# 16-head attention of the last layer: the maximum and its subtraction taken straight from PSUM by VectorE, without a copy of the scores and without GpSimd

## The chip, the cores and the metric

The kernel runs on one core of a Trainium2 chip. The metric is the device time of one execution in microseconds (us), the median of several runs. Five engines of the core work side by side, each through a queue of its own in program order, and they wait for one another through semaphores: PE (TensorE, the matrix engine), DVE (VectorE), ACT (ScalarE), POOL (GpSimd) and SP (SyncE, which issues transfers). SBUF is the on-chip memory, PSUM the memory into which PE writes its results, in 8 banks. POOL works on tiles in SBUF here and never on PSUM.

## The reference

The model has four layers, each a cross attention and a feed-forward part, over x of 2 x 512 x 128. The context has 2 x 77 x 128. Layer L2 (with a mask) and layer L3 (without one) use the same 16-head attention. L3, cut to what matters:

```python
def _L3_xattn_ref(query, key, value, Wq, bq, Wk, bk, Wv, bv, Wo, bo):
    H, D_K = 16, 8
    def proj(x, W, b):
        y = jnp.einsum('bsd,df->bsf', x, W) + b
        return y.reshape(B, -1, H, D_K).transpose(0, 2, 1, 3)
    q, k, v = proj(query, Wq, bq), proj(key, Wk, bk), proj(value, Wv, bv)
    scores = jnp.einsum('bhqd,bhkd->bhqk', q, k) / jnp.sqrt(jnp.float32(D_K))
    p = jax.nn.softmax(scores, axis=-1)
    x = jnp.einsum('bhqk,bhkd->bhqd', p, v)
    x = x.transpose(0, 2, 1, 3).reshape(B, -1, H * D_K)
    return jnp.einsum('bsd,df->bsf', x, Wo) + bo
...
x = x + _L3_xattn_ref(_layernorm(x, axis=-1), ctx_1024, ctx_1024, ...)
```

## The kernel before

Each engine has one function that writes out its whole program; nothing is scheduled by a planner, so the order on each queue is the order in which the code is written. `attention16(n, k)` stands once on each engine's side and is called twice: with n = 0 for L2 (mask) and n = 1 for L3 (no mask). It treats the 1024 queries in NT = 8 tiles of 128 rows. Batch b is t // 4. The scores of one tile are 16 heads x 77 keys = 1232 numbers in each of the 128 rows. They are computed as float32 split into high and low halves, three groups of four matmuls (L1091), and they fill banks 0 to 3 with 308 columns each.

What one tile goes through with n = 1:

- PE `scores(t)` writes banks 0 to 3. There is one such set of banks, so `scores(t + 1)` may begin only when `s16_taken` says that tile t has been copied away.
- DVE copies the 1232 columns to an SBUF tile `s16[z]` (L1944; three of them by turns; the profile calls them `shared` or `scratch`), counts `s16_taken`, and takes the negated maximum of each head from that SBUF copy into `neg_max16` (L1946), counting `max16_ok`.
- POOL `less_maximum` adds the negated maximum to `s16[z]` (L696) and counts `s16_ok`. With n = 0 a small operation on the maxima comes before (L694).
- ACT takes the exponential in two pieces (L1489, L1491; the profile calls the output `hT`).
- PE turns it in ten transposes (L1106, L1111), ACT copies these out (L1502, L1506; `w` in the profile), PE makes the weighted averages (L1122, L1126), ACT copies (L1479), PE turns back (L1134), DVE divides by the sum of the exponentials (L1956, L1959).

PE's queue works ahead of this by three tiles. First `scores(0)`, `scores(1)`, `scores(2)`, each of the last two behind a wait for the previous tile; then a loop over t, whose iteration is: wait for `s16_taken` of tile t + 2, `keep_warm(0, 1)` (one matmul of ones of 512 columns, two rows of 128x512 in the profile under L461, written to bank 0 and never used; its only purpose is to keep PE busy), `scores(t + 3)`, `averages(t - 1)`, `transposes(t)`, `turn_back(t - 1)`. In iteration 5 there are no scores left, but the wait for the last tile stays. Below, tile numbers are counted from 0, and "the filler" is the matmul of `keep_warm`.

Of the kernel before, what the change touches and what calls it, by code (L numbers as in the profile page):

```python
# [5 lines left out]
ALU = mybir.AluOpType  # L6
ACT = mybir.ActivationFunctionType
AX = mybir.AxisListType
# [5 lines left out]
P = 128  # L14
B = 2
NT = 8
# [20 lines left out]
def build(nc, a, out):  # L37
    S = a["x"].shape[1]
    D = a["x"].shape[2]
    NC = a["ctx_1024"].shape[1]  # L40
# [16 lines left out]
    BK = HM // 4  # L57
# [7 lines left out]
    with ExitStack() as ctx:  # L65
# [43 lines left out]
        for n in VROWS:  # L109
            k = vsrc[n].shape[0] // D  # L110
# [100 lines left out]
        s16 = [v.rearrange("p (h k) -> p h k", h=HM) for v in  # L211
               (scratch[:, 0:HM * NC], scratch[:, HM * NC:2 * HM * NC], shared[:, mask_at:mask_at + HM * NC])]
# [312 lines left out]
        def _(pool):  # L525
# [159 lines left out]
                            .then_inc(kv16_spread, 1)  # L685
                        nc.gpsimd.tensor_copy(to_left[:, :, :, DH], row_of).then_inc(kv16_spread, 1)

            def less_maximum(t, n):

                z = (NT * n + t) % 3  # L690
                pool.wait_ge(max16_ok, NT * n + t + 1)
                if n == 0:

                    own.add(nc.gpsimd.tensor_scalar(neg_max16[:, z, :], neg_max16[:, z, :], 1e37, None, ALU.min))  # L694
                    own.settle()
                nc.gpsimd.tensor_tensor(s16[z], s16[z], neg_max16[:, z, :].unsqueeze(2).to_broadcast([P, HM, NC]), ALU.add)\  # L696
                    .then_inc(s16_ok, 1)

# [30 lines left out]
            add_bias(4, bo16[:, 0, :])  # L729

            for t in range(NT):
                less_maximum(t, 0)
            spread_kv(1)
            inverse_root(5)

# [5 lines left out]
                    .then_inc(gu_product_ok, 1)  # L741
            inverse_root(6)
            add_bias(6, bo16[:, 1, :])
            for t in range(NT):
                less_maximum(t, 1)
            inverse_root(7)

        @block.tensor
        def _(pe):
# [322 lines left out]
            def attention16(n, k):  # L1072


                norm_transposes(k)

                def queries_of(b):
                    pe.wait_ge(xnT_b_ok[b], k)
                    nc.tensor.matmul(bank[:, 6 + b, :], w16[:, n, WQ, :], xnT[:, b, :], start=True, stop=True)\
                        .then_inc(q16_in_psum, 1)  # L1080

                def scores(t):
                    b, m = t // TPB, NT * n + t
                    pe.wait_ge(q16_ok, B * n + b + 1)
                    if t:
                        pe.wait_ge(s16_taken, m)
                    for stationary, moving in ((HI, HI), (HI, LO), (LO, HI)):
                        begin, end = stationary == moving, stationary == LO
                        for g in range(4):
                            rows = slice(32 * g, 32 * (g + 1))  # L1090
                            last = nc.tensor.matmul(bank[:, g, 0:BK * NC],  # L1091
                                                    qT[stationary][rows, b, (t % TPB) * P:(t % TPB + 1) * P],
                                                    k_blocks[moving][rows, b].rearrange("p h k -> p (h k)"),
                                                    start=begin, stop=end)
                    last.then_inc(s16_in_psum, 1)

                def transposes(t):

                    m, z = NT * n + t, t % 2
                    pe.wait_ge(p16_ok, 2 * (m + 1))  # L1100
                    if t:
                        pe.wait_ge(p16T_ok, 2 * m)
                    else:
                        pe.wait_ge(q16_ok, B * (n + 1))
                    for c in range(NPAIR):
                        last = nc.tensor.transpose(bank[:, 4 + c // 4, (c % 4) * P:(c % 4 + 1) * P],  # L1106
                                                   p16[:, z, 2 * PK * c:2 * PK * (c + 1)], ident[:])
                    last.then_inc(p16T_in_psum, 1)
                    for g in range(2):
                        first = HM * PK + LP * g  # L1110
                        last = nc.tensor.transpose(bank[0:LP, 6, g * P:(g + 1) * P], p16[:, z, first:first + LP],  # L1111
                                                   ident[:])
                    last.then_inc(p16T_in_psum, 1)

                def averages(t):

                    b, m = t // TPB, NT * n + t
                    pe.wait_ge(p16T_ok, 2 * m + 2)
                    if m >= 1:
                        pe.wait_ge(o16_ok, m)  # L1120
                    for g in range(2):
                        nc.tensor.matmul(bank[:, 7, g * P:(g + 1) * P], va_left[:, n, b, g, :], p16T[0:LP, NPAIR + g, :],  # L1122
                                         start=(g == 0), stop=False, skip_group_check=True)
                    for c in range(NPAIR):
                        g, rows = c // 4, slice(VW * (c % 4), VW * (c % 4 + 1))
                        last = nc.tensor.matmul(bank[rows, 7, g * P:(g + 1) * P], va_pair[:, n, b, c, :], p16T[:, c, :],  # L1126
                                                start=False, stop=(g == 1), skip_group_check=True)
                    last.then_inc(oT16_in_psum, 1)

                def turn_back(t):  # L1130

                    pe.wait_ge(oT16_ok, NT * n + t + 1)
                    for g in range(2):
                        last = nc.tensor.transpose(bank[:, 7, (2 + g) * P:(3 + g) * P], oT16[:, g, :], ident[:])  # L1134
                    last.then_inc(o16_in_psum, 1)

                def output_transposes(b):
                    for t in range(TPB * b, TPB * (b + 1)):
                        pe.wait_ge(o16_ok, NT * n + t + 1)
                        last = nc.tensor.transpose(bank[:, b, (t % TPB) * P:(t % TPB + 1) * P], o16[:, t, :], ident[:])  # L1140
                    last.then_inc(o16T_in_psum, 1)

                def output(b):
                    pe.wait_ge(o16T_ok, B * n + b + 1)
                    result_part(b, (3, 7)[b], lambda t: q16T[:, t // TPB, (t % TPB) * P:(t % TPB + 1) * P],
                                w16[:, n, WO, :])

                queries_of(0)
                keep_warm(4, 1)
                queries_of(1)  # L1150
                pe.wait_ge(kv16_spread, 7 * B * (n + 1))
                for t in range(3):
                    scores(t)
                for t in range(NT + 1):
                    if t + 3 < NT:
                        pe.wait_ge(s16_taken, NT * n + t + 3)
                        keep_warm(0, 1)
                        scores(t + 3)
                    elif t == NT - 3:
                        pe.wait_ge(s16_taken, NT * (n + 1))  # L1160
                        keep_warm(2, 1)
                    elif t == NT - 2:
                        output_transposes(0)
                        keep_warm(2, 1)
                    elif t == NT - 1:
                        output(0)
                        keep_warm(2, 1)
                    else:
                        keep_warm(2, 2)
                    if t:  # L1170
                        averages(t - 1)
                    if t < NT:
                        transposes(t)
                    if t:
                        turn_back(t - 1)
                keep_warm(2, 1)
                output_transposes(1)
                output(1)
# [416 lines left out]
        def _(dve):  # L1595
# [323 lines left out]
            def attention16(n, k, result):  # L1919
# [12 lines left out]
                for t in range(NT + LAG):  # L1932
                    m, z = NT * n + t, (NT * n + t) % 3
                    if t < NT:
                        scores, to = bank[:, 0:4, 0:BK * NC], s16[z].rearrange("p (g h) k -> p g (h k)", g=4)
                        dve.wait_ge(s16_in_psum, m + 1)
                        if m >= 3:
                            dve.wait_ge(p16_ok, 2 * (m - 2))
                        if n == 0:
                            nc.vector.scalar_tensor_tensor(out=to, in0=maskb[:, t, :].rearrange("p (g n) -> p g n", g=4),  # L1940
                                                           scalar=MASKED, in1=scores, op0=ALU.mult, op1=ALU.add)\
                                .then_inc(s16_taken, 1)
                        else:
                            nc.vector.tensor_copy(to, scores).then_inc(s16_taken, 1)  # L1944
                        dve.wait_ge(s16_taken, m + 1)
                        nc.vector.tensor_reduce(neg_max16[:, z, :], s16[z], AX.X, ALU.max, negate=True)\  # L1946
                            .then_inc(max16_ok, 1)
                    if t >= LAG:

                        d, y = NT * n + t - LAG, (t - LAG) % 2  # L1950
# [199 lines left out]
```

## Time and profile before

| | us |
|---|---|
| median of 3 runs | 504.54 |
| lowest and highest of them | 503.65, 505.76 |
| the profiled execution's own time | 503.58 |
| its span (first to last instruction) | 501.8 |
| outside the span in that execution | 1.78 |
| PE, DVE, ACT, POOL busy | 428.7, 345.4, 257.7, 132.3 |

Busy time tells how much work an engine has in sum, not who is waited for; for that one looks at the stage itself. L3's attention lies between about 386 and 432 us of the span: its first scores start at 386.81 us and the last tile's division (L1959) at 432.76 us. L2's attention lies between about 298 and 345 us and has the same shape.

### The profile page before, as it was taken

The numbers are of one execution on the slowest core, as the hardware profiler recorded it, in microseconds if no ns is written. First come the engines' busy times: TensorE is split into PE (matmuls) and PEld (weight loads), VectorE is DVE, ScalarE is ACT, GpSimd is POOL, SyncE is SP. The second block draws the span as 40 slices with busy tenths as digits, with TensorE's granted clock in tenths as the row PEclk, the third lists the DMA queues.
The fourth block names the chain that finished last, engine by engine and source line by source line (L and its number), as shares of the span: only waits on it lengthen the run. The fifth ranks groups of instructions, "written<-read, shape, count | busy, mean of one in ns | idle before, by whom it ended". The sixth has DMA issues, their size and how long they took to land.

```text
span 501.8 us, 8243 instructions
## 1 busy us (share of the span) xinstructions
PE 428.7 (85%) x2814; PEld 333.9 (67%) x2814; DVE 345.4 (69%) x767; ACT 257.7 (51%) x486; POOL 132.3 (26%) x196
## 2 busy tenths in 40 slices
PE   8989999999999999889998866998628699875095
PEld 5768989999999998679996634675214367532044
DVE  5658787777777776663338878835777883567983
ACT  3667766777766775453432133663441377225811
POOL 4530042403300000320105536682223552100000
PEclk9999999999999999998999997999957799988589
DMA  7789200000000000000000000000000000000001
GB/s 225 227 153 67 9 0 2 0 0 0 0 0 0 1 1 0 1 1 1 1 0 1 0 1 1 1 2 1 0 1 0 1 1 1 1 0 1 0 0 42
DMA packets 28456, 9.38 MB, mean 19 GB/s; under 512 B 17918, under 2 KB 27915, under 8 KB 28427
## 3 DMA queue, kind: packets, MB, share of 16 engines
q1 hardware_dynamic: 27164, 8.38, 10.2%
q10 hardware_dynamic: 1263, 0.61, 0.4%
q8 instruction: 17, 0.28, 0.3%
q14 instruction: 12, 0.10, 0.1%
HBM read 8.47 MB, written 0.52 MB: 18 GB/s over the span
## 4 chain that ended last, share of the span: by engine, by line
PE 69%; DVE 18%; issue 6%; ACT 4%; POOL 2%; POOLq 0%; DVEq 0%; ACTq 0%
PE bank L461 7%; PE bank L839 6%; PE bank L466 6%; PE bank L979 6%; PE bank L468 5%; PE bank L467 5%; PE bank L828 5%; PE bank L829 5%; PE bank L1106 3%; PE bank L860 3%; PE bank L1275 2%; PE bank L1122 2%; DVE stats L1610 2%; PE bank L1126 2%; PE bank L937 2%
## 5 line engine op out<-in xcount | busy, mean ns | idle before, releaser
L461 PE MATMUL bank<-ones 128*128 128x512 f32 x132 | 72.7, 677 | 4.9 <-POOL ident L531 1.8
L1685 DVE TENSOR_TENSOR probT_lo<-bank,probT_hi 128x512 fp32r<-128x512 f32 (+1 forms) x80 | 55.1, 688 | 23.7 <-ACT probT_hi L1363 23.6
L1363 ACT ACTIVATE probT_hi<-bank 128x512 fp32r<-128x512 f32 (+1 forms) x80 | 47.5, 593 | 42.8 <-PE bank L839 42.8
L1678 DVE TENSOR_REDUCE neg_max<-bank 128x1 f32<-128x589 f32 x64 | 49.1, 768 | 17.8 <-PE bank L829 16.6
L1354 ACT ACTIVATE shared<-bank,neg_max 128x589 f32<-128x589 f32 x64 | 47.9, 749 | 4.9 <-DVE neg_max L1678 4.8
L839 PE MATMUL bank<-ident,shared 128*128 128x128 f32 (+1 forms) x320 | 48.0, 272 | 0.4 <-ACT shared L1354 0.4
L607 POOL TENSOR_TENSOR rstd<-var_eps,minus_half 128x4 f32<-128x4 f32 x14 | 14.7, 1049 | 117.2 <-DVE var_eps L1616 117.2
L461 PEld LDWEIGHTS bank<-ones 128*128 128x128 f32 x132 | 25.8, 217 | 26.0 <-issue 19.8
L839 PEld LDWEIGHTS bank<-ident,shared 128*128 128x128 f32 (+1 forms) x320 | 39.8, 142 | 2.7 <-ACT shared L1354 0.6
L1858 DVE SCALAR_TENSOR_TENSOR x_residual<-bank,gate,x_residual 128x128 f32<-128x128 f32 x64 | 17.9, 344 | 24.0 <-PE bank L979 23.9
L466 PE MATMUL bank<-probT_hi,kv_lat_hi 128*128 128x512 f32 x64 | 30.9, 483 | 1.7 <-DVE probT_lo L1685 1.7
L979 PEld LDWEIGHTS bank<-w,hT 128*128 128x128 f32 x256 | 31.3, 201 | 0.6
L979 PE MATMUL bank<-w,hT 128*128 128x128 f32 (+1 forms) x256 | 31.6, 285 | 0.0
L562 POOL CAST a_now_hi<-ab 128x128 fp32r<-128x128 f32 x8 | 2.3, 290 | 99.8 <-PE bank L468 99.8
L1444 ACT ACTIVATE hT<-bank,vec_cols 128x512 f32<-128x512 f32 x24 | 16.4, 687 | 23.5 <-PE bank L468 23.5
L696 POOL TENSOR_TENSOR scratch<-scratch,neg_max 128x1232 f32<-128x1232 f32 x11 | 24.7, 2248 | 6.5 <-DVE neg_max L1946 6.0
L1068 PE MATMUL bank<-ident,pmax 128*128 128x128 f32 x14 | 3.7, 362 | 26.0 <-DVE pmax L1715 26.0
L468 PE MATMUL bank<-probT_hi,kv_lat_lo 128*128 128x512 f32 x64 | 25.2, 394 | 0.0
L467 PE MATMUL bank<-probT_lo,kv_lat_hi 128*128 128x512 f32 x64 | 25.1, 393 | 0.0
L1502 ACT ACTIVATE w<-bank 128x1024 f32<-128x1024 f32 x16 | 16.4, 1023 | 11.5 <-PE bank L1106 11.4
L1068 PEld LDWEIGHTS bank<-ident,pmax 128*128 128x128 f32 x14 | 2.4, 222 | 29.7 <-DVE pmax L1715 29.7
L828 PE MATMUL bank<-kvT_hi,qT_hi 128*128 128x296 f32 x64 | 19.5, 305 | 1.7 <-ACT shared L1354 1.2
(360 smaller groups left out, 1108.0 us busy)
## 6 DMA issues: line engine op xcount, KB each, us to landing
shared<-in_mask_Bx16xSxS_bk SPq DMA_DIRECT2D x8, 154.0 KB, 7.8
shared<-in_L_xattn_Wkv SPq DMA_DIRECT2D x8, 128.0 KB, 3.9
w<-in_L_ffn_W SPq DMA_DIRECT2D x1, 1024.0 KB
shared<-in_L_xattn_Wq SPq DMA_DIRECT2D x4, 128.0 KB, 3.8
x_residual<-in_x ACTq DMA_DIRECT2D x2, 256.0 KB, 4.8
shared<-in_L_xattn_Wo SPq DMA_DIRECT2D x4, 128.0 KB, 4.4
out_x<-x_residual SPq DMA_DIRECT2D x1, 512.0 KB, 3.2
wn<-in_L_ffn_w_gate SPq DMA_DIRECT2D x1, 192.0 KB, 3.7
```

What stands on the lines that cost most here:

```text
L461: nc.tensor.matmul(bank[:, at, :].rearrange("p (n m) -> p n m", n=4), ones[:], ones[:].unsqueeze(1).to_broadcast([P, 4, P]), start=True, s ...
L466: nc.tensor.matmul(out, lhsT[HI], rhs[HI], start=first, stop=False)
L467: nc.tensor.matmul(out, lhsT[HI], rhs[LO], start=False, stop=False)
L468: return nc.tensor.matmul(out, lhsT[LO], rhs[HI], start=False, stop=last)
L828: nc.tensor.matmul(left, q[stationary], kvT[moving][:, b, 0:HALF], start=begin, stop=end)
L829: last = nc.tensor.matmul(right, q[stationary], kvT[moving][:, b, HALF:wide], start=begin, stop=end)
L839: last = nc.tensor.transpose(bank[0:n, PT_BANK[b][c], i * P:(i + 1) * P], prob[b][:, i, c * P:c * P + n], ident[:])
L979: last = nc.tensor.matmul(bank[:, 6 + b, i * P:(i + 1) * P], hT[:, side, j, b, i * P:(i + 1) * P], w2[:, bass.ds(e, 1), j, :].rearrange("p ...
L1354: nc.scalar.activation(prob[b][:, i, :], scores0(i), ACT.Exp, bias=neg_max[:, b, i:i + 1], accum_out=row_sum[:, b, i:i + 1])\
L1363: nc.scalar.activation(probT[HI][0:n, SLOT[c], :], bank[0:n, PT_BANK[b][c], :], ACT.Copy)\
L1678: nc.vector.tensor_reduce(neg_max[:, b, i:i + 1], scores0(i), AX.X, ALU.max, negate=True)\
L1685: nc.vector.tensor_tensor(probT[LO][0:n, SLOT[c], :], bank[0:n, PT_BANK[b][c], :], probT[HI][0:n, SLOT[c], :].bitcast(F32), ALU.subtract). ...
```

## The change

With n = 1 (L3) alone, DVE takes the maximum of each head straight from banks 0 to 3, counts `max16_ok`, waits for its own result, and then adds the negated maximum to the scores, reading the banks a second time and writing `s16[z]`; it counts `s16_ok` itself. The copy L1944 and POOL's eight `less_maximum` of L3 are gone. PE, which waited for `s16_taken` before it wrote the banks again, now waits for `s16_ok` with n = 1. L2 stays as it was.

```diff
-            def less_maximum(t, n):
+            def less_maximum(t):
...
             for t in range(NT):
-                less_maximum(t, 0)
+                less_maximum(t)
...
-            for t in range(NT):
-                less_maximum(t, 1)
             inverse_root(7)
...
+                def scores_read(m):
+
+                    pe.wait_ge(s16_ok if n else s16_taken, m)
+
                 def scores(t):
                     b, m = t // TPB, NT * n + t
                     pe.wait_ge(q16_ok, B * n + b + 1)
                     if t:
-                        pe.wait_ge(s16_taken, m)
+                        scores_read(m)
...
                     if t + 3 < NT:
-                        pe.wait_ge(s16_taken, NT * n + t + 3)
+                        scores_read(NT * n + t + 3)
                         keep_warm(0, 1)
                         scores(t + 3)
                     elif t == NT - 3:
-                        pe.wait_ge(s16_taken, NT * (n + 1))
+                        scores_read(NT * (n + 1))
                         keep_warm(2, 1)
...
+                            dve.wait_ge(s16_taken, m + 1)
+                            nc.vector.tensor_reduce(neg_max16[:, z, :], s16[z], AX.X, ALU.max, negate=True)\
+                                .then_inc(max16_ok, 1)
                         else:
-                            nc.vector.tensor_copy(to, scores).then_inc(s16_taken, 1)
-                        dve.wait_ge(s16_taken, m + 1)
-                        nc.vector.tensor_reduce(neg_max16[:, z, :], s16[z], AX.X, ALU.max, negate=True)\
-                            .then_inc(max16_ok, 1)
+                            by_head = scores.rearrange("p g (h k) -> p g h k", h=BK)
+                            largest = neg_max16[:, z, :].rearrange("p (g h) -> p g h", g=4)
+                            nc.vector.tensor_reduce(largest, by_head, AX.X, ALU.max, negate=True).then_inc(max16_ok, 1)
+                            dve.wait_ge(max16_ok, m + 1)
+                            nc.vector.tensor_tensor(to.rearrange("p g (h k) -> p g h k", h=BK), by_head,
+                                                    largest.unsqueeze(3).to_broadcast([P, 4, BK, NC]), ALU.add)\
+                                .then_inc(s16_ok, 1)
```

On DVE, in L3's attention, tiles 3, 4 and 5 and the first division stand like this before (semaphores that a row waits for are in brackets):

```order
420 L1944 COPY shared<-bank 128x1232 [waits p16_ok,s16_in_psum]
421 L1946 TENSOR_REDUCE neg_max<-shared 128x16 [waits s16_taken]
422 L1944 COPY scratch<-bank 128x1232 [waits p16_ok,s16_in_psum]
423 L1946 TENSOR_REDUCE neg_max<-scratch 128x16 [waits s16_taken]
424 L1956 RECIPROCAL inv<-bank 128x16 [waits o16_ok,o16_in_psum]
425 L1959 TENSOR_TENSOR shared<-bank,inv 128x128 [waits dve_step]
426 L1944 COPY scratch<-bank 128x1232 [waits p16_ok,s16_in_psum]
```

and like this with the change (L1950 is the maximum, L1952 the addition):

```order
420 L1950 TENSOR_REDUCE neg_max<-bank 128x16 [waits p16_ok,s16_in_psum]
421 L1952 TENSOR_TENSOR shared<-bank,neg_max 128x1232 [waits max16_ok]
422 L1950 TENSOR_REDUCE neg_max<-bank 128x16 [waits p16_ok,s16_in_psum]
423 L1952 TENSOR_TENSOR scratch<-bank,neg_max 128x1232 [waits max16_ok]
424 L1963 RECIPROCAL inv<-bank 128x16 [waits o16_ok,o16_in_psum]
425 L1966 TENSOR_TENSOR shared<-bank,inv 128x128 [waits dve_step]
426 L1950 TENSOR_REDUCE neg_max<-bank 128x16 [waits p16_ok,s16_in_psum]
```

The number of large DVE operations per tile stays at two, but both now read the banks, and the banks are free after the second, not after the first.

On PE, in the same attention with the change, iterations 0 and 1 of the loop (scores of tiles 3 and 4; L1092 is the scores matmul, L1107 and L1112 the transposes, L461 the filler):

```order
850 L1092 MATMUL bank<-k_blocks_hi,qT_hi 128x308 [waits s16_ok,q16_ok]
851 L1092 MATMUL bank<-k_blocks_hi,qT_hi 128x308 x3
852 L1092 MATMUL bank<-k_blocks_lo,qT_hi 128x308 x4
853 L1092 MATMUL bank<-k_blocks_hi,qT_lo 128x308 x4
854 L1107 MATMUL bank<-ident,hT 128x128 [waits q16_ok,p16_ok]
855 L1107 MATMUL bank<-ident,hT 128x128 x7
856 L1112 MATMUL bank<-ident,hT 104x128 x2
857 L461 MATMUL bank<-ones 128x512 [waits s16_ok]
858 L1092 MATMUL bank<-k_blocks_hi,qT_hi 128x308 [waits s16_ok,q16_ok]
```

Before, rows 850, 857 and 858 waited for `s16_taken`. The order of PE's rows is the same; the filler stands behind the same wait as the scores, in front of everything else of its iteration.

## Rows read from the trace of the kernel before

**Rows 1.** The page, part 1: busy time, share, instructions of each engine.

```profile
PE 428.7 (85%) x2814; PEld 333.9 (67%) x2814; DVE 345.4 (69%) x767; ACT 257.7 (51%) x486; POOL 132.3 (26%) x196
```

**Rows 2.** Two stretches: start:end, length, PE, PEld, DVE, ACT, POOL, granted clock, DMA.

```profile
388.00:398.00 10.00, 4.42 (x34) 2.34 (x38) 8.73 (x7) 2.69 (x4) 5.57 (x3) 0.72 0.01 2
398.00:418.00 20.00, 19.91 (x209) 13.55 (x201) 16.21 (x18) 13.02 (x23) 10.76 (x6) 0.97 0.00 1
```

**Rows 3.** Chain that ended last, in order of time: start, length, what.

```profile
393.94 1.44 DVE scratch L1944
...
404.55 0.86 PE bank L461 x2
```

**Rows 4.** Timeline of the start, tiles 0 to 4: start, length, engine, line, operation.

```profile
388.30 1.43 DVE L1944 COPY shared<-bank 128x1232 f32<-128x1232 f32 x1
389.77 1.44 DVE L1946 TENSOR_REDUCE neg_max<-shared 128x16 f32<-128x1232 f32 x1
389.88 0.42 PE L1091 MATMUL bank<-k_blocks_hi,qT_hi 32*128 32x308 f32 x4 [2.37 <-DVE shared L1944]
...
392.70 0.63 PE L1091 MATMUL bank<-k_blocks_hi,qT_hi 32*128 32x308 f32 x4 [2.12 <-DVE scratch L1944]
393.56 1.07 ACT L1489 ACTIVATE hT<-shared 128x1024 f32<-128x1024 f32 x1 [5.96 <-POOL shared L696]
...
395.43 2.07 PE L461 MATMUL bank<-ones 128*128 128x512 f32 x2 [1.58 <-DVE scratch L1944]
...
397.43 0.63 PE L1091 MATMUL bank<-k_blocks_hi,qT_hi 32*128 32x308 f32 x4
...
398.50 1.45 PE L1106 MATMUL bank<-ident,hT 128*128 128x128 f32 x8
398.62 1.44 DVE L1944 COPY shared<-bank 128x1232 f32<-128x1232 f32 x1 [1.78 <-PE bank L1091]
...
400.12 1.13 PE L461 MATMUL bank<-ones 128*128 128x512 f32 x2
...
401.18 0.42 PE L1091 MATMUL bank<-k_blocks_hi,qT_hi 32*128 32x308 f32 x4
```

**Rows 5.** Timeline of one iteration in the steady part (scores of tile 5).

```profile
404.38 1.02 PE L461 MATMUL bank<-ones 128*128 128x512 f32 x2
...
405.34 0.41 PE L1091 MATMUL bank<-k_blocks_hi,qT_hi 32*128 32x308 f32 x4
...
406.08 1.44 DVE L1944 COPY scratch<-bank 128x1232 f32<-128x1232 f32 x1 [0.76 <-PE bank L1091]
...
408.55 1.02 PE L461 MATMUL bank<-ones 128*128 128x512 f32 x2
...
409.08 2.25 POOL L696 TENSOR_TENSOR scratch<-scratch,neg_max 128x1232 f32<-128x1232 f32 x1 [1.92 <-DVE neg_max L1946]
```

**Rows 6.** Timeline of the last scores (tile 7) and what follows.

```profile
413.66 0.41 PE L1091 MATMUL bank<-k_blocks_hi,qT_hi 32*128 32x308 f32 x4
...
416.87 1.02 PE L461 MATMUL bank<-ones 128*128 128x512 f32 x2
...
417.99 0.52 PEld L1122 LDWEIGHTS bank<-w,va_left 104*128 104x128 f32 x4 [0.92 <-ACT w L1506]
```

**Rows 7.** The page, part 5: DVE groups of other stages that read PSUM.

```profile
L1685 DVE TENSOR_TENSOR probT_lo<-bank,probT_hi 128x512 fp32r<-128x512 f32 (+1 forms) x80 | 55.1, 688 | 23.7 <-ACT probT_hi L1363 23.6
...
L1678 DVE TENSOR_REDUCE neg_max<-bank 128x1 f32<-128x589 f32 x64 | 49.1, 768 | 17.8 <-PE bank L829 16.6
```

**Rows 8.** A DVE operation in SBUF, one tensor and constants, from the timeline.

```profile
371.91 0.42 DVE L1980 TENSOR_SCALAR shared<-shared 128x512 f32<-128x512 f32 x1
```

**Rows 9.** Granted clock in short stretches; columns as in rows 2.

```profile
392.50:393.00 0.50, 0.30 (x4) 0.33 (x8) 0.47 (x2) 0.00 (x0) 0.50 (x1) 0.50 0.00 0
...
399.00:400.00 1.00, 1.00 (x9) 0.93 (x8) 1.00 (x1) 0.01 (x1) 0.17 (x1) 0.85 0.00 0
...
355.00:360.00 5.00, 3.77 (x17) 1.79 (x18) 2.95 (x9) 2.29 (x4) 0.12 (x1) 1.00 0.00 0
```

More of the change, by code:

```diff
@@ L686, in spread_kv @@
                         nc.gpsimd.tensor_copy(to_left[:, :, :, DH], row_of).then_inc(kv16_spread, 1)
-            def less_maximum(t, n):
[L690 to L695, printed above, removed]
+            def less_maximum(t):
+                z = t % 3
+                pool.wait_ge(max16_ok, t + 1)
+                own.add(nc.gpsimd.tensor_scalar(neg_max16[:, z, :], neg_max16[:, z, :], 1e37, None, ALU.min))
+                own.settle()
                 nc.gpsimd.tensor_tensor(s16[z], s16[z], neg_max16[:, z, :].unsqueeze(2).to_broadcast([P, HM, NC]), ALU.add)\
```

## The prediction

> **What bounds the kernel now.** I read the page first: PE is busy for 428.7 of 501.8 us, DVE for 345.4, POOL for 132.3 [rows 1]. This says that POOL is short of nothing, but not who is waited for in L3's attention, so the busy times of that stage come next. It has two parts. From 388 to 398 us DVE is busy for 8.73 of 10 us and PE for 4.42; from 398 to 418 us PE is busy for 19.91 of 20 us, DVE for 16.21 and POOL for 10.76 [rows 2]. The chain of work that ended last agrees: in the start it runs through DVE's copies, later through PE alone, the filler included [rows 3]. POOL's pass is on it nowhere in this stage.
>
> The timeline shows why. In the start PE sits idle before the scores of tiles 1 and 2 (2.37 and 2.12 us), released each time by DVE's copy [rows 4]: copy and maximum of a tile take DVE 2.82 us (388.30 to 391.12), and PE has nothing else in its queue yet. In the steady part one iteration takes 4.16 us (scores at 401.18 and 405.34) [rows 4, 5]. There DVE waits for PE (0.76 us idle before the copy), and POOL waits for DVE (1.92 us) [rows 5]. The number to watch is when the banks come free: the copy ends at 406.08 + 1.44 = 407.52, and PE's queue reaches the filler that wants bank 0 only at 408.55. So PE has about 1.0 us to spare, and a bank that is held longer than this stops PE.
>
> **The change part by part.** *POOL's eight passes* of 2.25 us go, 18.0 us of busy time. They are worth nothing: the exponential of tile 0 started at 393.56 and its two pieces take under 1.5 us, while PE reached the first transpose only at 398.50 [rows 4]. Later tiles have a whole iteration more in hand, since PE makes scores three tiles ahead. If this cover were gone the loss of POOL's pass would bring 2.3 us once (first rival).
>
> *DVE's work per tile.* Before: copy 1.44, maximum 1.44, with 0.03 between them for the wait on its own result (388.30 to 389.77) [rows 4]. Now: maximum from PSUM, addition from PSUM. No row shows either over 1232 columns. The maximum over 589 columns from PSUM took 768 ns and the difference of two operands over 512 columns, one in PSUM, 688 ns [rows 7]. Two such sizes differ by 77 columns and 80 ns, about one column a ns; what is left, 155 to 160 ns, is fixed. At 1.04 ns a column (the copy's 1.44 us fits 1232 x 1.04 + 155 = 1.44) both new operations come to 1.44 us. The bounds: a straight scaling of the maximum's row, 768 x 1232 / 589 = 1.61 us, from above, and from below an operation at the rate of the row in SBUF, 0.42 us for 512 columns [rows 8], which gives 155 + (420 - 155) x 1232 / 512 = 0.79 us. I take 1.44: reads from PSUM with two operands are at that rate in 80 rows. From the first scores read to the last it is then 1.44 + 0.03 + 1.44 = 2.91 us, and DVE's sum per tile is the same as before.
>
> The Trainium skill ("VectorE: DVE Perf Modes", the section on the TRN2 errata) gives an operation that reads PSUM 120 cycles beside its columns and one that reads SBUF 58, at 0.96 GHz. By this the maximum would cost some 65 ns more than before and the eight of them 0.5 us. The rows do not bear it out here: the maximum from SBUF over 1232 columns (1.44) and that from PSUM over 589 have the same fixed part, so the sum holds nothing for it. The same page's rules for authors say of elementwise work on a matmul's result that one should copy it to SBUF first if there will be many operations; with two readers the rule could be read against this change, and the reason here is one of waiting, which follows.
>
> *The banks are held for 2.91 us instead of 1.44.* This is what counts, since PE has one set of banks for the scores. Step by step, with the increments of before. From a release to the next scores there are 0.15 us (389.73 to 389.88); from a release to the filler 0.06 (400.06 to 400.12); from filler to scores 1.06 at full clock (400.12 to 401.18) and 2.00 at half (395.43 to 397.43); from the start of scores to DVE's start 0.74 at full clock (405.34 to 406.08) and 1.19 at half (397.43 to 398.62) [rows 4, 5].
>
> Scores 1: DVE starts on tile 0 at 388.30 as before and frees the banks at 391.21; scores 1 at 391.36, before 389.88, so +1.48. Scores 2: 391.36 + 0.74 + 2.91 + 0.15 = 395.16, before 392.70, +2.46. By then the granted clock has fallen; before, it was at half (1.2 of 2.4 GHz) from 392.5 on, after PE had done only one short burst of scores since about 387.5 (389.88 less the 2.37 us of idle time), and was full again within 399 to 400, some 4 us after the filler's start [rows 9]. Filler of tile 3: 395.16 + 1.19 + 2.91 + 0.06 = 399.32, before 395.43, +3.89. Scores 3: 401.32. The clock should come back around 403, so filler and scores 4 follow at full clock: 401.32 + 1.19 + 2.91 + 0.06 + 1.06 = 406.54, before 401.18, +5.36.
>
> From there a period is 0.74 + 2.91 + 0.06 + 1.06 = 4.77 us against 4.16, because the wait now ends 0.6 us after PE has run out of other work. Three periods to scores 7: 406.54 + 14.31 = 420.85 against 413.66, +7.19. The wait of iteration 5 stands behind tile 7 as well: the filler at 420.85 + 3.71 = 424.56 against 416.87, +7.69 [rows 6]. Then nobody waits for the banks. A little comes back: before, the averages after that filler waited for ACT until 417.99 [rows 6]; now ACT, which has run ahead, is done, and they start at about 424.56 + 1.06 = 425.6, +7.6. The rest of the kernel is unchanged.
>
> What is queued behind the longer wait on PE: filler, scores, averages, transposes, turning back, thus all of ACT's exponentials and DVE's divisions two iterations later; they move with PE and add nothing. DVE's own queue has maximum, addition, reciprocal and product; the last two take about 0.5 us (DVE is busy for 81% of a 4.16 us iteration [rows 2], 3.37 us, less 2.88 for the large two) and fit into the 1.9 us between a release and DVE's next start, in which PE does filler and scores.
>
> **The sum.** +7.6 us on the profiled execution's 503.58 gives 511.2. That execution is 0.96 us below the median; on the median the sum is 504.54 + 7.6 = 512.1 us.
>
> **The rivals.** (1) *POOL's pass was waited for, and its removal pays.* Place: tile 0, where ACT sat idle for 5.96 us before its first exponential, released by POOL [rows 4]. That exponential would start at 391.3 instead of 393.56, −2.3 us, 502.2. It decides if the exponential ends later than PE comes to the transposes; it ended at about 394.9 against 398.50, and PE comes later with the change. Chance 2 in 100. (2) *DVE's addition runs at the fast rate*, 0.79 us. Then a period is 0.74 + 2.26 + 0.06 + 1.06 = 4.12, no longer than before, and only the start loses: scores 1 at 390.71, scores 2 at 393.86, filler at 397.37, scores 4 at 403.94, +2.8 us, 507.3, at the border of what can be told. No row shows two operands, one in PSUM, at that rate, and 80 speak against it. Chance 4. (3) *The clock stays at half through the steady part*, because PE now waits 0.6 us in 4.8. A period is then at least 1.19 + 2.91 + 0.06 + 2.00 = 6.2 us and at most twice 4.16, 8.3, over four periods +6 to +14 us: 518 to 526. Against it: from 355 to 360 us PE was busy for 3.77 of 5 us, less than the 4.16 of 4.77 here, and the granted clock was full [rows 9]. Chance 4.
>
> The clock in the start is the open point within the forecast. In this kernel's rows the gap of 2.37 us before scores 1 left the clock full, and it had fallen by 392.5 [rows 4, 9]; scores 1 now come at 391.4, just ahead of that, after a gap of 3.8 us. If they are at half clock too, 0.45 us is added (512.6); I give this 3 in 10 within the forecast. The Trainium skill ("TensorE: Matmul & The Clock Gate", the table on why this matters for kernels) asks for no idle gaps between bursts of matmuls, or PE falls back to half clock. By that rule scores 1 would be at half clock and the time 512.6.
>
> **How the numbers follow.** Forecast 84 in 100, with these spreads: the clock not falling at all in the start, −0.45 − 0.94 − 0.45 = −1.8; scores 1 at half clock +0.45; the clock back an iteration late +1.4; the maximum at its upper bound +0.17 x 8 = +1.4; runs of the kernel before lie within 1.2 us of their median. That gives 509 to 515. Rivals 2, 4 and 4 in 100, and 6 for what I don't see. The range 508.7 to 515.3 leaves out the three rivals and little else. About 0.5% (2.5 us) is what a measurement of this kernel can tell from no change. Slower by more: 0.93; within: 0.05; faster: 0.02.
>
> **What would show it.** In the profile of the changed kernel: eight maxima and eight additions on DVE of 1.44 us each, and POOL idle in the stage. PE idle about 3.8 us before scores 1 and 0.6 us before each later filler, released by DVE's addition; four scores 4.77 us apart from tile 4 to tile 7; the stage of 398 to 418 us no longer 99% PE. The rest of the trace the same, some 7.6 us later. I'd be wrong if the addition is much off 1.44, if PE's filler turns out not to wait for the addition, or if the granted clock falls or rises at other places.

## The result, and the profile after

The changed kernel takes 514.98 us in the median of 4 runs (513.58 to 518.51), the kernel before 505.15 us beside it: a ratio of 1.0195, 95% interval 1.0151 to 1.0238, so 1.5 to 2.4% slower. A second series of the unedited changed kernel (below) gave 1.0182 (1.0128 to 1.0236). The forecast of 512.1 us against 504.54 is 1.0150: just below the lower end of the first interval and inside the second. The direction and the mechanism are as forecast. The measured loss, 9.8 us between the medians of the first series and 8.0 in the second (515.21 against 507.17), is somewhat larger than the 7.6 us of the sum.

First the page after, parts 1 and 4:

```profile
PE 436.1 (85%) x2814; PEld 338.4 (66%) x2814; DVE 345.9 (67%) x767; ACT 257.7 (50%) x486; POOL 114.3 (22%) x188
...
PE 66%; DVE 21%; issue 5%; ACT 4%; POOL 2%; DMA 1%; ACTq 1%; POOLq 0%; DVEq 0%
```

POOL is busy for 18.0 us less than in [rows 1], DVE for almost the same time (345.9 us against 345.4). Nothing was gained from it. The timeline of the attention without mask shows why; first the start (tiles 0 to 4; columns as in [rows 4], to which it answers):

```profile
391.24 1.43 DVE L1950 TENSOR_REDUCE neg_max<-bank 128x16 f32<-128x1232 f32 x1
392.70 1.44 DVE L1952 TENSOR_TENSOR shared<-bank,neg_max 128x1232 f32<-128x1232 f32 x1
394.18 1.07 ACT L1490 ACTIVATE hT<-shared 128x1024 f32<-128x1024 f32 x1 [3.64 <-DVE shared L1952]
...
394.29 0.41 PE L1092 MATMUL bank<-k_blocks_hi,qT_hi 32*128 32x308 f32 x4 [3.85 <-DVE shared L1952]
...
398.10 0.63 PE L1092 MATMUL bank<-k_blocks_hi,qT_hi 32*128 32x308 f32 x4 [3.12 <-DVE scratch L1952]
...
402.26 2.07 PE L461 MATMUL bank<-ones 128*128 128x512 f32 x2 [3.02 <-DVE scratch L1952]
404.27 0.63 PE L1092 MATMUL bank<-k_blocks_hi,qT_hi 32*128 32x308 f32 x4
...
405.34 1.97 PE L1107 MATMUL bank<-ident,hT 128*128 128x128 f32 x8
...
408.44 2.07 PE L461 MATMUL bank<-ones 128*128 128x512 f32 x2 [0.70 <-DVE shared L1952]
...
410.44 0.63 PE L1092 MATMUL bank<-k_blocks_hi,qT_hi 32*128 32x308 f32 x4
```

The exponential of tile 0 is indeed ready early (394.18, 2.94 us after DVE's start; before it was 5.26 us). PE comes to the transposes that need it only at 405.34. In front of scores 1 and 2 and the first filler PE is idle for 3.85, 3.12 and 3.02 us, each time until DVE's addition; before it was 2.37, 2.12 and 1.58. Then one iteration of the steady part and the filler after the last scores, which answer to [rows 5, 6]:

```profile
424.16 1.12 PE L461 MATMUL bank<-ones 128*128 128x512 f32 x2 [0.35 <-DVE shared L1952]
...
425.22 0.42 PE L1092 MATMUL bank<-k_blocks_hi,qT_hi 32*128 32x308 f32 x4
...
425.97 1.44 DVE L1950 TENSOR_REDUCE neg_max<-bank 128x16 f32<-128x1232 f32 x1 [1.37 <-ACT hT L1492]
...
427.44 1.44 DVE L1952 TENSOR_TENSOR scratch<-bank,neg_max 128x1232 f32<-128x1232 f32 x1
...
428.94 1.12 PE L461 MATMUL bank<-ones 128*128 128x512 f32 x2 [0.35 <-DVE scratch L1952]
```

From filler to filler it is 4.78 us (424.16 to 428.94), before 4.17. In front of each of these fillers PE now waits for DVE, which it did not do before; DVE still waits for PE's scores, as it did. The wait shows as 0.35 us of idle time, not as the 0.6 that the prediction named as its sign, although the period has grown by the full 0.61. The rest is overlap that is lost: before, a filler started 0.16 us ahead of the end that the profile gives the row in front of it (L1134 ended at 417.03, the filler began at 416.87), and a filler that had to wait is followed by the scores after 1.06 us, one that had not after 0.96. The releaser named before DVE's maximum is ACT, but its row ends within 0.04 us of the scores (425.95 and 425.91), and the distance from scores to DVE's start is 0.75 us as before; so it is the scores that DVE waits for.

For the rest I measure the stage by itself, so that what happens ahead of it does not count: from DVE's first read of tile 0's scores to the first addition to x after the attention. Before it is 388.30 to 429.28, 40.98 us; after 391.24 to 441.10, 49.86 us, so +8.88. The two spans differ by 12.4 us; the other 3.5 us lie outside the stage: 2.94 ahead of it, in code that no edit touches, and 0.58 behind. In nine profiles of kernels that differ only in this stage its start lay between 388.06 and 394.13 us. The granted clock is the likely cause: its mean ahead of the stage was 0.96 in the four profiles in which the stage started at 388.06 to 390.13 us, 0.95 in the four with 391.24 to 393.96, and 0.94 in the one with 394.13. In each profile it is at half for some microseconds, at different places. Two windows, of the kernel before and then of the changed one (columns as in [rows 2]), show places where only the changed kernel's clock had fallen; from 220 to 230 us it was the other way round (0.83 before, 1.00 changed):

```profile
200.00:210.00 10.00, 7.35 (x38) 5.38 (x38) 6.81 (x27) 3.94 (x7) 4.25 (x6) 1.00 0.00 0
...
280.00:290.00 10.00, 8.82 (x52) 6.07 (x51) 8.69 (x34) 3.29 (x8) 3.56 (x9) 1.00 0.00 0
```

```profile
200.00:210.00 10.00, 8.12 (x31) 6.33 (x31) 6.42 (x27) 2.66 (x5) 4.25 (x6) 0.71 0.00 0
...
280.00:290.00 10.00, 8.84 (x44) 6.62 (x44) 7.22 (x31) 2.16 (x5) 3.71 (x9) 0.83 0.00 0
```

### The profile page after: what moved, and what is told of

Read it like the earlier page. It is cut to its first block, busy times and chain, and to the rows that moved or that the text cites. A ratio compares the mean times of both kernels' runs of the same rounds, so it can differ in the third digit from the quotient of the medians.

```text
span 514.2 us, 8235 instructions
## 1 busy us (share of the span) xinstructions
PE 436.1 (85%) x2814; PEld 338.4 (66%) x2814; DVE 345.9 (67%) x767; ACT 257.7 (50%) x486; POOL 114.3 (22%) x188
## 4 chain that ended last, share of the span: by engine, by line
PE 66%; DVE 21%; issue 5%; ACT 4%; POOL 2%; DMA 1%; ACTq 1%; POOLq 0%; DVEq 0%
PE bank L836 6%; PE bank L461 6%; PE bank L466 6%; PE bank L468 5%; PE bank L467 5%; PE bank L976 5%; PE bank L825 4%; PE bank L826 4%; PE bank L857 3%; PE bank L1107 2%; PE bank L1276 2%; PE bank L1092 2%; DVE stats L1611 2%; DVE neg_max L1950 2%; PE bank L1123 1%
## 5 line engine op out<-in xcount | busy, mean ns | idle before, releaser
L461 PE MATMUL bank<-ones 128*128 128x512 f32 x132 | 74.5, 691 | 8.2 <-DVE scratch L1952 3.7
L461 PEld LDWEIGHTS bank<-ones 128*128 128x128 f32 x132 | 26.3, 221 | 31.0 <-issue 20.3
L976 PEld LDWEIGHTS bank<-w,hT 128*128 128x128 f32 x256 | 29.7, 192 | 0.6
L976 PE MATMUL bank<-w,hT 128*128 128x128 f32 (+1 forms) x256 | 30.0, 275 | 0.0
L934 PE MATMUL bank<-ident,xn 128*128 128x128 f32 x56 | 13.5, 330 | 8.6 <-DVE xn L1773 3.9
```

Source lines behind the costliest of these rows:

```text
L461: nc.tensor.matmul(bank[:, at, :].rearrange("p (n m) -> p n m", n=4), ones[:], ones[:].unsqueeze(1).to_broadcast([P, 4, P]), start=True, s ...
L976: last = nc.tensor.matmul(bank[:, 6 + b, i * P:(i + 1) * P], hT[:, side, j, b, i * P:(i + 1) * P], w2[:, bass.ds(e, 1), j, :].rearrange("p ...
```

## The experiments

**The hold alone.** Copy, maximum in SBUF and POOL's pass stay; only PE is released later, by the maximum instead of the copy, with n = 1.

```diff
-                        pe.wait_ge(s16_taken, m)
+                        pe.wait_ge(max16_ok if n else s16_taken, m)
...
-                        pe.wait_ge(s16_taken, NT * n + t + 3)
+                        pe.wait_ge(max16_ok if n else s16_taken, NT * n + t + 3)
...
-                        pe.wait_ge(s16_taken, NT * (n + 1))
+                        pe.wait_ge(max16_ok if n else s16_taken, NT * (n + 1))
```

> The kernel before, but PE waits in the attention without mask for the maximum of a tile and not for its copy before it writes the banks again; copy, maximum and POOL's subtraction stay. The stage is measured from DVE's first read of tile 0's scores to the first addition to x after the attention (before: 388.30 to 429.28, 40.98 us; changed kernel: 391.24 to 441.10, 49.86 us). Theory (the longer hold of the banks is the whole loss): the banks are held for 2.91 us here too, so the stage takes 49 to 50 us, the run some 8 to 10 us more than before, the same as the changed kernel. Rival (the loss comes from reading PSUM twice or from DVE's new operations): stage 41 us, time as before. Rival (POOL's absence is worth something): stage over 50 us, longer than the changed kernel's by up to 2.3 us.

Measured: ratio 1.0173 (1.0105 to 1.0241). The stage runs from 390.13 to 438.55, 48.42 us, +7.44, a little under the 49 to 50 us expected. The filler of tile 4 came at full clock here (1.13 us), in the changed kernel at half (2.07):

```profile
390.13 1.43 DVE L1944 COPY shared<-bank 128x1232 f32<-128x1232 f32 x1
...
401.14 2.07 PE L461 MATMUL bank<-ones 128*128 128x512 f32 x2 [3.01 <-DVE neg_max L1946]
...
407.31 1.13 PE L461 MATMUL bank<-ones 128*128 128x512 f32 x2 [1.67 <-DVE neg_max L1946]
...
438.55 0.68 DVE L1803 TENSOR_TENSOR x_residual<-bank,x_residual 128x512 f32<-128x512 f32 x1
```

So the longer hold of the banks alone makes nearly the whole loss, with POOL at work and a single read of PSUM. What is missing to the changed kernel's 49.86, 1.44 us, looks like the clock, and two runs below test this.

**Subtraction on DVE, in SBUF, without the hold.**

```diff
                         nc.vector.tensor_reduce(neg_max16[:, z, :], s16[z], AX.X, ALU.max, negate=True)\
                             .then_inc(max16_ok, 1)
+                        if n:
+                            dve.wait_ge(max16_ok, m + 1)
+                            nc.vector.tensor_tensor(s16[z], s16[z], neg_max16[:, z, :].unsqueeze(2)
+                                                    .to_broadcast([P, HM, NC]), ALU.add).then_inc(s16_ok, 1)
```

The eight `less_maximum(t, 1)` of POOL are taken out as well.

> The kernel before, but in the attention without mask DVE subtracts the maximum itself, in SBUF, after copy and maximum; POOL's pass is gone and PE is released by the copy as before. Theory (hold of the banks): no loss from the hold; but DVE has 4.37 us of large operations a tile plus 0.5 us of division against an iteration of 4.16 us, so DVE becomes the bound: the start loses 1.45 us a tile and the stage takes 45 to 47 us, 4 to 6 us more than before, less than the changed kernel. Rival (that POOL's pass is waited for): the stage would be shorter than 40.98 us.

Measured: ratio 1.0126 (1.0062 to 1.0191), stage 394.13 to 442.36, 48.23 us, +7.25 where 4 to 6 was expected. DVE is the bound, with no idle time between these rows of its timeline (the copy is L1942, the maximum L1944, the new addition L1948):

```profile
416.51 1.43 DVE L1942 COPY scratch<-bank 128x1232 f32<-128x1232 f32 x1
417.97 1.44 DVE L1944 TENSOR_REDUCE neg_max<-scratch 128x16 f32<-128x1232 f32 x1
419.44 1.44 DVE L1948 TENSOR_TENSOR scratch<-scratch,neg_max 128x1232 f32<-128x1232 f32 x1
420.80 0.25 DVE L1958 RECIPROCAL inv<-bank 128x16 f32<-128x16 f32 x1
421.08 0.29 DVE L1961 TENSOR_TENSOR shared<-bank,inv 128x128 f32<-128x128 f32 x1
421.29 1.43 DVE L1942 COPY shared<-bank 128x1232 f32<-128x1232 f32 x1
```

4.78 us from copy to copy. The copy of the last tile starts 31.94 us after the first, before 26.11, so +5.8 by then. What the expectation left out comes behind it: the averages after the filler of iteration 5 wait for a division that now stands behind the third pass on DVE's queue, and the stage ends 1.4 us later still:

```profile
431.09 0.68 PE L1120 MATMUL bank<-w,va_left 104*128 104x128 f32 x4 [1.21 <-DVE shared L1961]
```

So POOL's pass was off the path, but not useless: given to DVE as a third pass it costs about as much as the hold does (7.25 and 7.44 us, one profile each, both with the clock at half for part of the start). The changed kernel pays with the banks what this one pays with DVE's time.

**The filler out of the way of the release.** From the changed kernel, with n = 1 alone:

```diff
                         scores_read(NT * n + t + 3)
-                        keep_warm(0, 1)
+                        if n == 0:
+                            keep_warm(0, 1)
                         scores(t + 3)
...
                         averages(t - 1)
+                    if t + 3 < NT and not (n == 0):
+                        keep_warm(4, 1)
                     if t < NT:
```

> The changed kernel, but in the attention without mask the filler of iterations 0 to 4 stands between the averages and the transposes and is written to bank 4, so it does not wait for the release of banks 0 to 3 and is not between the release and the scores. Theory (loss = held banks plus the filler queued behind the release): from scores 4 on an iteration is PE's own 4.16 us again instead of 4.78, and scores 3 come 1.9 us earlier; the stage takes 45 to 46 us instead of 49.86. Rival (DVE's two passes bound the iteration by themselves): the period stays at 4.7 to 4.8 us and the stage at 48 us or more.

Measured: ratio 1.0125 (1.0071 to 1.0179), stage 388.06 to 434.44, 46.38 us, 3.48 less than the changed kernel's and just above what was expected. Most of the gain is in the start, where scores 3 came 1.92 us and scores 4 3.76 us earlier than in the changed kernel, in part because the clock was back sooner (scores 4 took 0.41 us here, 0.63 there). From scores 5 on the period was 4.60 us (scores 408.32 to 412.92), not 4.16. There PE no longer waits for DVE, but for ACT: with the filler between averages and transposes only the turning back and the scores are left between the transposes and the averages that need ACT's copies of them, and the filler lies in the ring of transposes, ACT's copies and averages:

```profile
408.32 0.41 PE L1092 MATMUL bank<-k_blocks_hi,qT_hi 32*128 32x308 f32 x4
...
409.34 0.71 PE L1123 MATMUL bank<-w,va_left 104*128 104x128 f32 x4 [0.32 <-ACT w L1510]
...
412.92 0.41 PE L1092 MATMUL bank<-k_blocks_hi,qT_hi 32*128 32x308 f32 x4
```

A bound of 4.7 to 4.8 us by DVE's two passes is not what this period shows, and a later run with a period of 3.81 us refutes it outright; that the loop would return to PE's own 4.16 us is refuted here.

**The clock kept up in the start.** From the changed kernel:

```diff
                 for t in range(3):
                     scores(t)
+                    keep_warm(4, 3 if n else 0)
```

> The changed kernel, but in the attention without mask three fillers to bank 4 stand behind each of scores 0, 1 and 2, where PE is idle for 3.85, 3.12 and 3.02 us. Theory: the wait for the banks is the same, but the granted clock stays full, so scores 2, 3 and 4 and the fillers of tiles 3 and 4 run at full clock: 0.45 us three times and 0.95 us twice come back, stage 46 to 47 us instead of 49.86, with the period of 4.78 us from tile 4 on unchanged. Rival (the clock is not what made the start longer than forecast): stage 49 to 50 us.

Measured: ratio 1.0111 (1.0062 to 1.0161), stage 392.82 to 439.44, 46.62 us, 3.24 less, as expected, with the steady period unchanged (scores 404.45, 409.24, 414.00). The window of the whole stage, columns as in [rows 2], has the granted clock at full:

```profile
392.82:439.44 46.62, 41.79 (x365) 26.61 (x364) 26.43 (x31) 23.36 (x40) 0.00 (x0) 1.00 0.00 1
```

**The changed kernel again,** unedited.

> The changed kernel once more, unedited, for a second profile and more times. Theory: what the first profile had above the sum (stage 8.9 us longer where 7.6 were worked out) is the granted clock coming back one iteration late, which depends on chance: the stage takes either about 48.4 us (clock back before the filler of tile 4) or 49.9; the start of the stage, in code that no edit touches, lies anywhere from 388 to 394 us of the span as in the profiles so far. Ratio to before 1.015 to 1.020. Rival (the 1.4 us belong to the change itself): stage 49.9 again, with the filler of tile 4 at half clock.

Measured: ratio 1.0182 (1.0128 to 1.0236). The stage runs from 393.96 to 444.26, 50.30 us: neither of the two lengths expected. This time scores 1 came at half clock too (0.63 against 0.41 us in the first profile), after the same gap:

```profile
397.01 0.63 PE L1092 MATMUL bank<-k_blocks_hi,qT_hi 32*128 32x308 f32 x4 [3.84 <-DVE shared L1952]
...
411.61 2.08 PE L461 MATMUL bank<-ones 128*128 128x512 f32 x2 [0.70 <-DVE shared L1952]
```

The filler of tile 4 was at half clock again. Of itself this run can't tell chance from the change, and the rival expectation had this filler right. The next run takes the clock out of the comparison.

**The hold alone, clock kept up.** From the kernel with the hold alone, with the three fillers of above.

```diff
                     scores(t)
+                    keep_warm(4, 3 if n else 0)
```

> The kernel before with the banks released by the maximum in the attention without mask (as in the run with the hold alone) and three fillers to bank 4 behind each of its scores 0, 1 and 2 (as in the run of the changed kernel with the clock kept). With the clock at full in both, this one has copy, POOL's pass and the hold, the other the two reads of PSUM and no POOL. Theory (hold alone, POOL worth nothing): the stage takes 46.6 us within 0.2, as the changed kernel with the clock kept (46.62). Rival (POOL's pass is waited for once): 48.9 us. Rival (reading PSUM twice costs something): less than 46.4 us.

Measured: stage 391.70 to 438.26, 46.56 us, against 46.62 of the changed kernel with the same fillers (one execution, 513.10 us). The window of its whole stage, to be read against the one two runs above:

```profile
391.70:438.26 46.56, 41.78 (x365) 26.60 (x364) 26.39 (x31) 23.36 (x40) 17.98 (x8) 1.00 0.00 1
```

With the clock out of it, a kernel that copies, reads PSUM once and uses POOL and one that reads PSUM twice and does not use POOL take the same time within 0.06 us. So the 1.44 us between the changed kernel and the hold alone went with the clock, not with reading PSUM twice or with POOL.

**Fillers at the start of the kernel before,** in both attentions.

```diff
                     scores(t)
+                    keep_warm(4, 2)
```

> The kernel before with two fillers to bank 4 behind each of scores 0, 1 and 2, in both 16-head attentions, where PE is idle for 2.4, 2.1 and 1.6 us. Theory: the granted clock stays full, filler and scores of tile 3 and the first transposes run at full clock; scores 2 at half clock cost nothing there, since DVE is the one waited for; the stage without mask takes 39.1 to 39.5 us instead of 40.98, the run some 3 to 4 us less. Rival: the clock falls anyway or the fillers come in the scores' way: 41 us or more.

Measured: ratio 0.9987 (0.9945 to 1.0028), inconclusive as a time; stage 388.80 to 428.40, 39.60 us, −1.38, a little less than expected, with the clock at full through the stage. The runs scatter by 5 to 6 us (503.2 to 508.9, and 503.3 to 509.7 for the kernel before beside it), so that a gain of 1.4 us in each of two stages cannot be told from none.

This run also gives the price of the hold without the clock on either side. With the clock at full in both, the stage takes 39.60 us with the banks released by the copy and 46.56 and 46.62 us with the longer hold: the hold costs 7.0 us. Of the 8.88 us between the two profiles of the unedited kernels the other 1.9 are the clock's, which takes 1.4 us of the stage before and 3.2 us of the changed one.

**No filler in the loop of the kernel before,** with the fillers at the start, in both attentions.

```diff
                     scores(t)
+                    keep_warm(4, 2)
...
-                        keep_warm(0, 1)
+                        keep_warm(0, 0)
```

> As the run with fillers at the start of the kernel before, and the filler of iterations 0 to 4 left out in both attentions. PE's own work in an iteration is then 3.2 us, and the ring transposes, ACT's copies, averages, transposes takes about 3.6 us. Theory: period 3.6 to 3.7 us instead of 4.16, scores 4 come 2.7 us earlier, the clock stays full since PE is busy for over 80%; stage without mask 36.5 to 37.5 us instead of 40.98, the run 7 to 9 us less than before, 497 us. Rival (the clock needs the filler): the granted clock falls within the stage and the stage takes over 41 us.

Measured: ratio 0.9877 (0.9811 to 0.9944), 499.14 us where 497 was expected; stage 384.88 to 422.06, 37.18 us, −3.80, as expected. The last period is 3.69 us (scores 402.35 to 406.04), with PE waiting for ACT; the three before it were 2.82, 3.31 and 4.12 us, the longest with PE waiting 0.77 us for DVE's division. The clock was at full (columns as in [rows 2]):

```profile
384.00:394.00 10.00, 9.12 (x62) 4.52 (x58) 9.68 (x8) 2.56 (x5) 5.00 (x3) 1.00 0.01 2
394.00:410.00 16.00, 13.70 (x178) 10.83 (x178) 15.24 (x17) 12.46 (x23) 10.97 (x6) 1.00 0.00 1
```

**The same once more.**

> The version with fillers at the start and none in the loop, both attentions as in the kernel before otherwise, unedited once more: stage without mask 37.2 us again with the granted clock at full, ratio to before 0.983 to 0.990, from two stages that are 3.8 us shorter each. Rival (the first profile was lucky with the clock): a stage of 38 us or more with the clock at half somewhere in it.

Measured: 498.05 us, ratio 0.9843 (0.9796 to 0.9889), stage 388.93 to 426.11, 37.18 us again, with the clock at full. By the intervals of the two series this version is 0.6 to 1.9% and 1.1 to 2.0% faster than the kernel before.

**No filler in the loop of the changed kernel,** n = 1 alone, with the fillers at the start.

```diff
                     scores(t)
+                    keep_warm(4, 3 if n else 0)
...
-                        keep_warm(0, 1)
+                        keep_warm(0, 0 if n else 1)
```

> The changed kernel with three fillers to bank 4 behind each of scores 0, 1 and 2 and without the filler of iterations 0 to 4, in the attention without mask alone. Theory (the loss is the hold of the banks plus what stands between release and scores): a period is 0.74 + 2.91 + 0.15 = 3.80 us instead of 4.78, the stage takes 41.5 to 42.5 us instead of 49.86, about 1 us above the kernel before; the run about 506 us. Rival (DVE's two passes or reads of PSUM cost by themselves): period above 4.5 us, stage above 45. Rival (the clock needs the filler): the clock falls in the stage.

Measured: ratio 1.0035 (0.9993 to 1.0077), 508.85 us where about 506 was expected; stage 388.91 to 431.69, 42.78 us, 7.1 less than the changed kernel's and 0.3 above the upper end expected. The period is 3.81 us (scores 408.19, 412.00, 415.81), as worked out. The excess goes with the clock, which fell once in the stage; here the rival that the clock needs the filler came true in part. These windows show the fall, after PE had been idle for 1.87 us before scores 4 (403.39):

```profile
402.00:403.00 1.00, 0.00 (x0) 0.00 (x0) 1.00 (x1) 1.00 (x3) 0.00 (x0) 1.00 0.00 0
403.00:404.00 1.00, 0.61 (x12) 0.55 (x12) 0.25 (x1) 0.87 (x2) 0.00 (x0) 0.86 0.00 0
...
406.00:407.00 1.00, 1.00 (x15) 0.62 (x5) 1.00 (x1) 0.38 (x1) 0.00 (x0) 0.50 0.00 0
```

and from scores 4 to scores 5 it took 4.80 us (403.39 to 408.19) instead of 3.81. Even so reshaped, the changed stage is 5.6 us longer than the stage of the kernel before reshaped in nearly the same way (37.18 us, with two fillers instead of three behind each of the first scores); 1.0 of them is this fall of the clock.

## Why the prediction was right

Point by point, by its own steps. Times are in us from DVE's first read of tile 0's scores, first those worked out in the prediction (its times less 388.30), then measured:

| | predicted | hold alone | changed | changed again |
|---|---|---|---|---|
| scores 1 | 3.06 | 3.05 | 3.05 | 3.05 |
| scores 2 | 6.86 | 6.85 | 6.86 | 7.31 |
| filler of tile 3 | 11.02 | 11.01 | 11.02 | 11.47 |
| scores 4 | 18.24 | 18.23 | 19.20 | 19.65 |
| scores 7 | 32.55 | 32.54 | 33.98 | 34.42 |
| filler of iteration 5 | 36.26 | 36.26 | 37.70 | 38.14 |
| first addition to x | 48.6 | 48.42 | 49.86 | 50.30 |

*POOL's passes are worth nothing:* right, and shown by the two runs with the clock kept up. *Maximum and addition from PSUM cost 1.44 us each:* right to 0.01 us, and rival 2 (a fast addition) is refuted. By the Trainium skill ("VectorE: DVE Perf Modes", the section on the TRN2 errata) the maximum from PSUM would take 65 ns more than from SBUF, as the prediction worked out from its cycles. The runs do not show this: over 1232 columns it takes 1.43 to 1.44 us from either. *The longer hold costs 7.6 us:* right; alone it was 7.44, and 7.0 with the clock at full on both sides. The chain of increments, from release to scores, to DVE, to release, holds in each step. *What comes back from ACT at the end* was 0.25 us (the filler of iteration 5 came 7.69 us later in the run with the hold alone, the end of the stage 7.44), where the prediction had 0.1. *PE idle 0.6 us before each later filler:* the period grew by that, but the idle time shown is 0.35 us. Rival 1 is refuted, and rival 3 too: in the changed kernel's steady part the clock was full.

What was off is a size. The forecast took the clock to come back "around 403", before the filler of tile 4. In both profiles of the changed kernel it came back one iteration later. Scores 3 still stood where they were worked out in the first of them (13.03 us, predicted 13.02); then the filler of tile 4 took 0.95 us more, and DVE's start after scores 4 came 0.45 us later than at full clock. That is the "+1.4" which the prediction had among its spreads, not in its sum. In the second profile scores 1 came at half clock as well (the "+0.45", given 3 in 10): 7.44 + 1.44 + 0.44 = 9.3 us, which is what the stage took more. The second ratio gives 0.0182 x 507 = 9.2 us, but its interval reaches from 6.5 to 12.0, and the code ahead of the stage varies by several us from run to run, so that this agreement proves little. That the clock is not fixed by the program is shown for scores 1 alone, at full in one profile of the changed kernel and at half in the other. Its late return came in both of these profiles, and the hold alone, in its one profile, had the clock back in time after nearly the same gaps: whether that was chance or has to do with the program stays open. The rest of the first profile's 12.4 us lay ahead of and behind the stage.

The measured time lies near the upper end of the stated range. The sum accounts for 7.6 of the 9.8 us between the medians, and a spread, not the sum, for the 1.4 us of the late clock. The code ahead of the stage moved the stage's start by up to 6 us in nine profiles; the prediction had this only as 1.2 us around the median of the kernel before. That it did not carry the time out of the range is luck.

## What to carry to other kernels

Before an operation is moved from a copy to its PSUM source, count how long the banks are held by it, not how many operations it saves: what counts is the time from the release to the next release against the time in which PE has other work. Here 1.47 us more hold met 0.9 us of slack, and the period grew by 0.6 us. POOL was busy for 26% and off the path: its eight passes cost nothing there, and taking them away gained nothing, while the same passes on DVE cost 7.25 us. Whether a filler that is to keep PE's clock up pays has to be tried out, and where it stands as well: behind the awaited release it lengthened the loop, and between averages and transposes it lengthened the ring through ACT's copies. Without it, and with a few fillers in the idle gaps of the start, the attention of the kernel before took 3.8 us less, of which the fillers at the start gave 1.4. The one profile of the changed kernel shaped like this lost 1.0 us again to a fall of the clock.

## What the hardware showed

In both profiles of the kernel before without the filler in the loop the granted clock was 1.00 through 16 us of the loop, in which PE was busy for 13.70. In the changed kernel without it the clock fell from 1.00 to 0.50 at about 403.7 us, after 1.87 us without work on PE; in the two kernels with start fillers and the filler in the loop it stayed at 1.00 after the same kind of gap (1.78 us).

The clock's fall differed from run to run after the same work and the same gap: after 3.85 us without work scores 1 ran at full clock in one profile of the changed kernel (0.41 us) and at half in the other (0.63). Its return differed between kernels: counted from the start of the first filler (11.0 us after DVE's start), the clock was back 3.3 us later with the hold alone and about 10 us later in both profiles of the changed kernel. Of the first of these (half through 411 to 412, 0.84 in 412 to 413):

```profile
411.00:412.00 1.00, 1.00 (x14) 0.69 (x7) 0.36 (x1) 0.00 (x0) 0.00 (x0) 0.50 0.00 0
412.00:413.00 1.00, 1.00 (x20) 0.78 (x19) 1.00 (x1) 0.00 (x0) 0.00 (x0) 0.84 0.00 0
```

In between PE was idle for only 0.70 us. DVE took 1.43 to 1.44 us for 1232 float32 columns in each of these: copying them out of PSUM, taking the maxima from PSUM or SBUF, and adding the broadcast maxima from PSUM or SBUF. POOL took 2.25 us for that addition in SBUF.
